# Two output products of TensorE ahead of the state products, in twelve groups of a linear attention

## What is computed

```python
def _L0_attn_ref(x, ...):
    xn = _layer_norm(x, ln_g, ln_b)
    q, k, v = split(xn @ qkv_w + qkv_b)
    gate = sigmoid(xn @ gate_w + gate_b)
    k = elu(k * gate) + 1.0
    q = elu(q) + 1.0
    attn = einsum('btd,bsd->bts', q, k) * tril(ones((T, T)))
    out_num = einsum('bts,bsd->btd', attn, v)
    out_den = sum(q * cumsum(k, axis=1), axis=-1) + DEN_EPS
    return out_num / out_den

def _L0_ffn_ref(x, ...):
    scores = (x @ router_w.T + router_b) / temp
    gates = _sinkhorn(scores)                  # three rounds
    topk_vals, topk_idx = top_k(gates, 2)
    all_out = (relu(x @ wg) * (x @ wp)) @ wo   # per expert
    return x + sum(gathered * topk_gates)

x = x + _L0_attn_ref(xn, ...) + _L0_ffn_ref(xn, ...)
```

## Time and profile before

| | us |
|---|---|
| median of 3 runs | 388.4 |
| lowest and highest run | 387.77, 388.95 |
| span of the profiled execution | 387.7 |
| TensorE busy | 346.6 |
| VectorE busy | 271.5 |
| GpSimd busy | 267.4 |
| ScalarE busy | 235.4 |

### The profile page before, as it was taken

How to read it: one execution, slowest core, us unless ns; L and a number is a source line. 1 busy time by engine, 2 the same in 40 slices (tenths; PEclk the granted TensorE clock), 3 DMA queues, 4 the chain that set the end, 5 groups by cost and what they waited for, 6 DMA issues and landing times.

```text
span 387.7 us, 8994 instructions
## 1 busy us (share of the span) xinstructions
PE 346.6 (89%) x2632; PEld 311.0 (80%) x2632; DVE 271.5 (70%) x745; ACT 235.4 (61%) x442; POOL 267.4 (69%) x363
## 2 busy tenths in 40 slices
PE   0779799799989888999999999999999999999880
PEld 0769568667768777786699999999999999999770
DVE  3998789998798888774266666676656666666440
ACT  3679644126756655653268777777767777775530
POOL 3696999947877544647065777777756777777773
PEclk9999999969999999999999999999999999999996
DMA  6999999997424323259467677677674555563330
GB/s 181 253 315 334 336 334 266 319 248 225 137 100 146 116 82 98 94 157 310 112 170 191 191 214 210 183 223 212 174 207 116 160 135 164 140 170 106 93 103 0
DMA packets 64287, 70.98 MB, mean 183 GB/s; under 512 B 6099, under 2 KB 59103, under 8 KB 64241
## 3 DMA queue, kind: packets, MB, share of 16 engines
q1 hardware_dynamic: 53968, 48.56, 47.6%
q0 software_dynamic: 8672, 21.19, 15.0%
q10 hardware_dynamic: 1600, 0.67, 0.7%
HBM read 28.54 MB, written 43.04 MB: 185 GB/s over the span
## 4 chain that ended last, share of the span: by engine, by line
PE 68%; DVE 16%; issue 6%; POOL 4%; DMA 3%; ACT 2%; SPq 0%; ACTq 0%; POOLq 0%; DVEq 0%
PE psum L1652 15%; PE psum L1639 7%; PE psum L1640 7%; PE psum L1641 7%; PE psum L1617 4%; PE psum L1459 3%; PE psum L1521 3%; PE psum L1629 3%; POOL out L551 3%; PE psum L1350 2%; DVE stats L844 2%; PE psum L1441 2%; DMA rows<-in_L_attn_x 2%; PE psum L1403 2%; PE psum L1444 2%
## 5 line engine op out<-in xcount | busy, mean ns | idle before, releaser
L537 POOL DMA_INDIRECT by_upper<-row x70 | 69.0, 985 | 35.0 <-issue 15.1
L529 POOL DMA_INDIRECT by_lower<-rows,slot_u x64 | 64.5, 1008 | 36.0 <-DVE rows L960 19.2
L551 POOL DMA_INDIRECT out<-row x70 | 68.8, 983 | 25.7 <-issue 15.9
L1652 PE MATMUL psum<-w_expert,hT 128*128 x560 | 76.9, 277 | 1.0 <-DVE hT L1283 0.5
L1639 PE MATMUL psum<-xT_high,w_now 128*128 128x256 f32 x232 | 70.2, 303 | 0.8 <-issue 0.8
L1652 PEld LDWEIGHTS psum<-w_expert,hT 128*128 128x128 f32 x560 | 69.4, 192 | 1.8 <-issue 1.6
L748 ACT ACTIVATE w_now<-w_split 128x1024 fp32r x58 | 61.4, 1058 | 15.4 <-PE psum L1641 15.4
L1641 PE MATMUL psum<-xT_high,w_now 128*128 128x256 f32 x232 | 65.5, 282 | 0.0
L1640 PE MATMUL psum<-xT_low,w_now 128*128 128x256 f32 x232 | 65.4, 282 | 0.0
L1287 DVE TENSOR_TENSOR hT<-relu,psum 128x512 f32<-128x512 f32 x58 | 39.9, 687 | 34.7 <-PE psum L1641 31.3
L1295 DVE SCALAR_TENSOR_TENSOR row<-psum,row 128x128 f32<-128x128 f32 x140 | 43.6, 346 | 9.6 <-PE psum L1652 1.5
(11 more groups left out here) (256 smaller groups left out, 697.4 us busy)
## 6 DMA issues: line engine op xcount, KB each, us to landing
by_lower<-blank SPq DMA_DIRECT2D x1, 10140.0 KB, 34.8
by_upper<-blank SPq DMA_DIRECT2D x1, 10062.0 KB, 72.7
row<-by_lower SPq DMA_DIRECT2D x29, 260.0 KB, 3.4
row<-by_upper SPq DMA_DIRECT2D x29, 258.0 KB, 3.1
rows<-in_L_attn_x SPq DMA_DIRECT2D x8, 512.0 KB, 9.5
row<-by_upper SPq DMA_DIRECT2D x12, 129.0 KB, 2.2
row<-by_lower SPq DMA_DIRECT2D x11, 130.0 KB, 2.4
by_upper<-row POOLq DMA_INDIRECT x70
```

What stands on the lines that cost most here:

```text
L529: pool.indirect_dma_start(by_lower, bass.IndirectOffsetOnAxis(ap=slot_u[:, t:t + 1], axis=0), rows[:, t, :], None).then_inc(scattered, 16)
L537: pool.indirect_dma_start(by_upper, bass.IndirectOffsetOnAxis(ap=row[:, q, k, SLOT_UP:SLOT_UP + 1].bitcast(U32), axis=0), row[:, q, k, 0:R ...
L551: pool.indirect_dma_start(out_rows, bass.IndirectOffsetOnAxis(ap=row[:, q, k, TOKEN:TOKEN + 1].bitcast(U32), axis=0), row[:, q, k, BASE], ...
L1652: last = pe.matmul(psum[:, 4 + n % 2, k * D:(k + 1) * D], hT[:, n % 3, f, k * P:(k + 1) * P], weights, start=(f == 0), stop=(f == FB - 1))
```

## The change

In TensorE's loop, for groups 3 to 14, the output products of tile 1 are issued ahead of the third state product, and those of tile 2 ahead of the fourth. The router's product of group three stays between tile 1 and tile 2. Group 15, which leaves the loop before these lines, and groups 0 to 2 keep their order, and no other engine's list changes. The order before was: state 1, output 0, state 2, output 1, state 3, output 2, output 3 (tiles counted from 0). It is now: state 1, output 0, output 1, state 2, output 2, state 3, output 3.

```diff
@@ -1591,12 +1591,12 @@
                 project(n + 1, "q")
                 add_state(n, 1)
                 out_chunk(n, 0)
+                out_chunk(n, 1)
                 add_state(n, 2)
-                out_chunk(n, 1)
-                add_state(n, 3)
                 if n == EARLY:
                     route_wide()
                 out_chunk(n, 2)
+                add_state(n, 3)
                 out_chunk(n, 3)
```

## The result

The changed kernel takes 385.19 us in the median (12 runs, 383.53 to 387.15), the kernel before 387.32 in 12 runs measured with it (385.73 to 389.54). The ratio of the runs is 0.9933, with a 95% interval from 0.9911 to 0.9955, and that of the two medians is 0.9945: faster by 2.1 us by the medians and by 1.7 to 3.4 by the interval. The forecast was 386.3 with a range from 385.2 to 388.0. The gain of 2.1 us is as forecast, but the time lies 0.01 us under the range. What failed is the level that the gain was taken from: 388.4 for a kernel whose runs have their median at 387.3.

A forecast was written before the change was run, and what follows sets the result against it. TensorE was taken to bound the attention stage except where VectorE's keys come later, with 4.7 us of waits for saved states. 4 x 0.45 + 2 x 0.15 = 2.1 us off 388.4 gave 386.3, range 385.2 to 388.0.

The forecast's parts named there:

- The level: Whole kernel: the shown median of 388.4 us, 0.7 above the profiled span of 387.7, from which the gain was taken.
- The lower end of my range: Whole kernel: 385.2 us, allowing another 0.4 us from late keys coming earlier and a spread of 0.6 in the runs.
- The sum of 2.1 us: Attention groups: 0.45 us each in 3, 4, 10 and 12, net 0.15 each in 7 and 13.
- the slow first product: Next group's scores: where they begin with a wait for keys, the first product costs 0.11 us, leaving net 0.15 of 0.26.
- the selection of groups: Attention stage: gain in groups 3, 4, 7, 10, 12 and 13; none in 5, 6, 8, 9, 11 and 14.
- rival (a): Odd groups: tile 1 delays the third state product by 0.17 us; gain 1.7 us, time 386.7; chance 0.16.
- the 0.10: Odd groups: third state product ending 0.10 us earlier if its weights load while tile 1 runs; not counted.
- One reading behind it: TensorE: a first product after a wait takes 0.49 us against 0.39, as a weight load standing behind the wait would look.
- rival (b): End of attention: the gain stops at GpSimd's scatter queue and the expert stage starts as today; 388.4 us, chance 0.13.
- rival (c): TensorE's clock falls to half at the longer wait before score six, 1.64 us; 1.1 us slower, 389.5; chance 0.06.
- I priced a fall at half of its length: TensorE: 6.5 us at half clock would lose up to 3.2 us.

The follow-up runs named there:

- E9: The kernel before with 49 unread products on TensorE, 19 at 76 to 78 us and 30 ahead of group three's scores: 386.95 us, ratio 0.9982.
- E10: The changed kernel with 49 unread products on TensorE, 19 at 76 to 78 us and 30 ahead of group three's scores: 385.01 us, ratio 0.9928.
- E2: Against the kernel before, the new order in groups 3, 4, 7, 10, 12 and 13 alone: 385.08 us, ratio 0.9937.
- E3: Against the kernel before, the new order in groups 5, 6, 8, 9, 11 and 14 alone: 387.11 us, ratio 1.0002.
- E5: Against the kernel before, output products of the second and third tile both ahead of the third state product, groups 3 to 14: 387.35 us, ratio 1.0004.
- E7: The kernel before with 19 unread products on TensorE at 76 to 78 us: 387.96 us, ratio 1.0014.
- E8: The changed kernel with 19 unread products on TensorE at 76 to 78 us: 386.26 us, ratio 0.9954.
- E1: The changed kernel again without edit, beside the kernel before on the same chip: 385.15 us, ratio 0.9937.
- E6: The changed kernel with VectorE's weight split of groups 5, 9 and 11 moved behind the operation that makes the keys: 383.31 us, ratio 0.9897.
- E12: The changed kernel with 49 unread products; weight splits (groups 5, 9, 11) and last table operations (groups six, eight) behind the keys: 381.72 us, ratio 0.9854.
- E4: Against the kernel before, only the second tile's output products ahead of the third state product, groups 3 to 14: 386.13 us, ratio 0.9974.

## Why the prediction was wrong, and where it was right

**The level: the step that failed.** The prediction said "The median shown is 388.4, 0.7 above that span, within its runs", and took the gain off it. The median of those three runs was 388.4, that of all 12 runs measured beside the changed kernel 387.32, and that of the other nine 387.19. The experiments have 387.36 in 89 runs. So the level was 1.1 us too high: three runs are few for a kernel whose runs lie between 385.0 and 390.7. With 387.3 as the level the forecast is 385.2. The lower end of my range left 0.4 for the gain and 0.6 for the spread of runs (which makes 385.3, where I wrote 385.2), and nothing for a level 1.1 us off.

A sign of this was read wrongly, though it is no term of the sum. A run's time is not 0.7 but 1.8 us above its span: 384.96 against 383.2 in the profiled execution after, and 1.75 to 1.83 in the medians of every kernel whose runs list both. So the profiled execution before, with its span of 387.7, was by this estimate one of about 389.5 us, at the slow end of its kernel's runs. Its time is given nowhere, but a granted clock of 0.50 for some 6.5 us stood in the earlier trace rows. That the gain came out at 2.1 us and still missed the range by only 0.01 is a matter of chance, as the medians move by more than that.

**What moves the level.** Of the 89 runs, 34 have a mean clock of 0.9875 or more and a median of 386.63, 55 have less and a median of 387.77: 1.1 apart, as much as the fall cost between scores two and three in the profile before. By round they are 0.8, 1.8 and 0.1 apart (387.88 and 387.98 in the third). So the fall may explain a part. That it does is not shown, since E9, in which the mean clock is high in all runs, is not clear of the kernel before (0.9982, interval to 1.0002), and it isn't known what spreads runs of the same clock over 2 us and more.

**The change itself.** The sum of 2.1 us was right in its parts. Expected and measured periods of groups three to fourteen: 6.7, 6.6, 8.0, 7.3, 6.5, 7.6, 7.5, 6.8, 7.7, 6.7, 6.4, 6.5 against 6.81, 6.68, 8.03, 7.27, 6.53, 7.63, 7.49, 6.76, 7.71, 6.76, 6.42, 6.51. None is off by more than 0.11, and that one is group three. Its scores now begin with a wait, which costs the slow first product, and in the profile before they did not, because the clock had fallen. This is also about half of the difference between 2.1 and the 1.87 of the stretch. Where both kernels wait there, in E9 and E10, group three goes from 7.26 to 6.80. E2 and E3 show that the selection of groups was right, and not merely the total.

**The late state product,** rival (a), fell: 4.32 us against 4.31. The starts tell what TensorE can take up, the recorded durations overlap. E5 shows that there was room for one tile and not for two. The rule of the Trainium skill, "TensorE: Matmul & The Clock Gate", section "Part 2: What happens when you issue a matmul", that weight loads are pulled ahead, is seen in E5, where the product waited for nothing (0.39 us), but not across a wait in the changed kernel (0.48 us). So it was right not to count the 0.10. One reading behind it was too broad: a record of 0.49 stands not only behind a listed wait, but also where none is listed (143.43 in the earlier trace rows).

**The scatters,** rival (b), moved with the keys of group fifteen and kept their idle time in front, 1.77 us.

**The clock,** rival (c), was not a danger where I put it: the wait before score six, 1.62 to 1.64 us in six profiles, left it at 1.00 in all of them. It was real elsewhere. In E7 and E8 a wait of 1.9 us was followed by a fall, and in four other profiles the same wait was not. I priced a fall at half of its length. That came out where TensorE's own pace counts: the windows of E7 add up to 3.4 us at the lower clock, and group three took 1.6 longer. Ahead of score three VectorE's late keys hide a part, as TensorE would have waited 1.9 us there. The fall in the profile before cost 1.1 us, and the longer one in E1, to 88 us, cost 2.5 (18.25 - 15.79).

## What to carry to other kernels

Before a gain is worked out for filling a wait, write down for each round of the loop the two times that the next step waits for; only the rounds in which the filled engine is the later one pay, here 2.1 of 5.4 us, and afterwards the other engine is what to work on (E6 gave 1.8 us more of the stretch, E12 another 1.0). How much fits into a wait is read from the starts of the instructions, not from their durations. And a forecast of an absolute time needs the level of the profiled execution as well: look for a stretch of low clock in it before setting it equal to the median.

## What the runs showed of the hardware

- A fall of TensorE's clock to 0.50, that is 1.2 of 2.4 GHz, came behind a place from 76 to 78 us in which it was busy 1.11 of 2.00, and in two profiles behind a wait of 1.9 us. With fillers in both places it did not come there in any of the four profiles that have them. Without them the same places were passed at 1.00 in the profile after and in E2, E4 and E5, so it comes in some executions of a kernel and not in others.
- Filling one thin place is not enough. In both profiles that have the first place filled alone a fall came at 86 us, where it cost 1.6 us and not 1.1 (E7, E8). That these kernels are slower for it is not shown (E7: 1.0014, 0.9985 to 1.0043).
- The product behind a 128x129 product of 32-bit numbers starts 0.22 us after it, and 0.32 us after it if that one had waited for another engine; the record of the one that had waited is 0.10 us longer, 0.49 for 0.39.
